# Key parts stored sooner, one bias waited for later, another loaded a stage earlier

## The chip, the cores and the metric

One core of one Trainium2 chip runs the whole program in one launch. The metric is the device time of that launch in microseconds (us); the time given for a kernel is the median over its runs.

## What is computed

Four pairs of layers on x (4 x 512 tokens, width 256): a cross attention against a second sequence `ctx`, then a feed-forward part. Each layer adds to x. What matters here are these three:

```
# L1 ffn: expert choice, 32 experts, each takes its top 8 of the rows of a (4, 32, 512) gating table
h = gelu(selected @ w1[e] + w1_last_row[e])        # 256 -> 1024
o = h @ w2[e] + w2_last_row[e]                     # 1024 -> 256, scattered back onto x
# keys of the L2 and L3 attentions depend on ctx alone
kL2 = rope(ctx @ WkL2.T);   kL3 = ctx @ WkL3.T + bk
# L3 attention: 16 heads of 16, values
v = ctx @ WvL3.T + bv
scores = scores * clip(exp(sqrt((tot - cumsum(softmax)) * |i-j|) * gamma * diff))
out = softmax(scores) @ v
```

## The kernel before

The program is written engine by engine with hand-set semaphores; each stage is a block that ends in a barrier of all engines. The order of the work on each engine is the order in which it is written. The stages stand in this order: attention L0x, experts L0f, attention L1x, experts L1f (`expert_choice`), attention L2x, experts L2f (`top2_experts`), distance attention L3x (`distance_layer`), feed-forward L3f.

**Stage L1f, the loop over experts.** 32 experts are taken in 8 groups g of 4. Each expert has two weights of 1024 KB, `w1s` in a ring of 8 buffers and `w2s` in a ring of 4. For each group PE computes `up(g)` (L2255), turns h (`turn`, L2268), and computes `down(g)` (L2281); ACT copies the left half of h (L2316) and applies Gelu (L2327); DVE copies the right half (L2347), adds the first bias (L2354) and, after `down(g)`, adds the second bias `b2` into `stage` (L2363). SP issues the loads: the `w2s` of group g once `down(g-1)` is done, then the `w1s` of group g+1 (L2100, L2096). The `w1s` of groups 0 and 1 and the `w2s` of group 0 were asked for in the stage's opening. `b2` (8 groups x 256 values for every partition, 1024 KB) is asked for when the loop begins, and DVE waits for it at the very beginning.

**Keys made beside it.** The class `LaterKeys` uses PE's free time for 16 jobs, the keys of L2x (jobs 0 to 7, rotated by angle) and of L3x (jobs 8 to 15). `project(j)` on PE; `take(j)` on ACT; `split(j)` on DVE writes two of three bf16 parts; `last_part(j)` on POOL writes the third (L2073) and signals `lo_done`; `store(j)` on ACT waits for `lo_done` and issues a DMA of 384 KB (L1998). The parts lie in a ring of 4, so `take(j)` (L2032) waits until the store of job j-4 has landed. Each group has at most three jobs:

```
between, first, second = ([None] * 5 + [9, 12, 15], [None, 1, 3, 5, 7, 10, 13, None],
                          [0, 2, 4, 6, 8, 11, 14, None])
```

`between[g]` is projected between `up(g)` and `turn(g)`, `first[g]` before `down(g)`, `second[g]` after it. Before the change ACT stores, in group g right after the copy of h, the jobs second[g-2], between[g-1] and first[g-1].

**The distance layer.** `norm_and_project` opens it: SP issues the load of the value bias `bv` and then of `wk` and `bk`; PE waits for `bv` before the first value product (L320), and ACT waits for `bv`, `wk` and `bk` before it issues four loads of 1024 KB into `apart` (L2862), whose sigmoids (L2872) it computes between copies. `distance_attention` then runs a software pipeline over 64 heads of 4 tiles each. Its small tiles (`nm1`, `rl`, `mx2`, `nm2`, `gate`, `v_sum_pair`, `pick`, `rdm`) each have memory of their own; each holds between 4 and 68 values a partition.

Of the kernel before, what the change touches and what calls it, by code (L numbers as in the profile page):

```python
# [2076 lines left out]
def expert_choice(c, ks2, ks3, wv2):  # L2077
# [6 lines left out]
    with ExitStack() as ctx:  # L2084
# [105 lines left out]
        with ExitStack() as ectx:  # L2190
# [20 lines left out]
            with nc.Block() as block:  # L2211
# [98 lines left out]
                def _(act):  # L2310
                    act.wait_ge(hT_cleared, 1)
                    for g in range(G):
# [4 lines left out]
                        if g:  # L2317
                            for j in (second[g - 2] if g > 1 else None, between[g - 1], first[g - 1]):
                                if j is not None:
                                    later.store(act, j)  # L2320
                            later.leading(act, second[g - 1])
# [3 lines left out]
                        if g >= 1:  # L2325
                            act.wait_ge(o_done, g)
                        nc.scalar.activation(hT[:, :, :, 0:B], hb[:], ACT.Gelu  # L2327
                                             ).then_inc(g_done, 1)
                        if first[g] is not None:
                            later.take(act, first[g])  # L2330
                            later.leading(act, first[g])
                        if second[g] is not None:
                            later.take(act, second[g])
                    later.store(act, second[G - 2])
                    later.store(act, between[G - 1])
# [4 lines left out]
                def _(dve):  # L2340
                    dve.wait_ge(b1_loaded, 16)
                    dve.wait_ge(b2_loaded, 16)
                    for g in range(G):
# [16 lines left out]
                        if between[g] is not None:  # L2360
                            later.split(dve, between[g])
                        dve.wait_ge(o_done, g + 1)
# [141 lines left out]
def top2_experts(c, wv3):  # L2504
# [14 lines left out]
    with ExitStack() as ctx:  # L2519
# [187 lines left out]
        with ExitStack() as gctx:  # L2707
# [8 lines left out]
            with nc.Block() as block:  # L2716
# [11 lines left out]
                def _(pe):  # L2728
# [3 lines left out]
                    pe.wait_ge(wv3_loaded, 16)  # L2732
# [182 lines left out]
def distance_attention(c, tag, stacks, vaug, o_dram, mask, apart, gamma, room_v, ahead):  # L2915
# [17 lines left out]
    with ExitStack() as ctx:  # L2933
        nm1 = c.sb(ctx, tag + "nm1", [P, F], F32)
        rl, mx2, nm2 = (c.sb(ctx, tag + n, [P, F], F32) for n in ("rl", "mx2", "nm2"))
# [38 lines left out]
        with nc.Block() as block:  # L2974
# [24 lines left out]
            def _(pe):  # L2999
# [43 lines left out]
                def turn_back(g, q):  # L3043

                    pe.wait_ge(oT_copied, g + 1)
                    for t in range(TB):
                        to = op[:, t * 2 * VW:(t + 1) * 2 * VW]
                        nc.tensor.matmul(to, oT[:, t * P:(t + 1) * P], pick[:].rearrange("p h d -> p (h d)"),
# [146 lines left out]
            def _(dve):  # L3195
# [50 lines left out]
                def invert(g):  # L3246

                    dve.wait_ge(o_done, g + 1)
                    nc.vector.reciprocal(rdm[:], o4[:, :, :, dk]).then_inc(rd_done, 1)

                def outputs(g):
# [6 lines left out]
                                                  rdm[:].unsqueeze(3).to_broadcast([P, TB, 2, dk]), ALU.mult)  # L3258
# [26 lines left out]
def distance_layer(c, ks, wv):  # L3285
# [6 lines left out]
    with ExitStack() as ctx:  # L3292
# [8 lines left out]
        with ExitStack() as wctx:  # L3301
# [3 lines left out]
            bv = c.sb(wctx, tag + "bv", [P, HD], F32)  # L3305
# [8 lines left out]
            def other_loads(sp):  # L3314
                sp.dma_start(bv[:], dram["L3_bv"].partition_broadcast(P)).then_inc(v_loaded, 16)
# [11 lines left out]
            def mask_terms(dve, made):  # L3327
# [4 lines left out]
                             (v_loaded, 16), None, (wk, wk, wv), (bks, bk, bv), 0.25, (qs, ks), vaug, dk + 1,  # L3332
# [3 lines left out]
        distance_attention(c, tag, stacks, vaug, o_dram, (mq, am, vsum), apart, gamma, wv, ahead)  # L3336
# [14 lines left out]
def build(nc, dram, out, layers):  # L3351
    with ExitStack() as ctx:
# [20 lines left out]
        if "L3x" in layers:  # L3373
            with ExitStack() as w_ctx:
                wv3 = c.sb(w_ctx, "L3x_wv", [P, KD, D], F32)
                top2_experts(c, wv3)
                c.end_layer()
                distance_layer(c, ks3, wv3)
# [101 lines left out]
```

## Time and profile before

| | us |
|---|---|
| median of 3 runs | 3150.31 |
| lowest and highest run | 3141.8, 3152.29 |
| the profiled execution | 3181.4 |
| its span, first to last instruction | 3179.6 |
| stage L1f within the span | 1288.4 to 1511.5 |
| opening of L3x within the span | 2307.2 to 2369.7 |

PE was busy 2735.3 us of the span (86%), DVE 1879.2 (59%), ACT 1720.9 (54%), POOL 851.0 (27%). Times in the rows are microseconds from the start of the span unless marked ns. PE is the matrix engine, PEld its weight loads, DVE the vector engine, ACT the scalar engine, POOL the general one; SPq and ACTq are the queues in which SP and ACT issue DMAs. L2281 is line 2281 of the kernel. "[3.67 <-PE ...]" at a row's end is the engine's idle time before it and what ended that.

### The profile page before, as it was taken

The numbers are of one execution on the slowest core, as the hardware profiler recorded it, in microseconds if no ns is written. First come the engines' busy times: TensorE is split into PE (matmuls) and PEld (weight loads), VectorE is DVE, ScalarE is ACT, GpSimd is POOL, SyncE is SP. The second block draws the span as 40 slices with busy tenths as digits, with TensorE's granted clock in tenths as the row PEclk, the third lists the DMA queues.
The fourth block names the chain that finished last, engine by engine and source line by source line (L and its number), as shares of the span: only waits on it lengthen the run. The fifth ranks groups of instructions, "written<-read, shape, count | busy, mean of one in ns | idle before, by whom it ended". The sixth has DMA issues, their size and how long they took to land. (4 is left out here: it accounts for less than half of the span.)

```text
span 3179.6 us, 43427 instructions
## 1 busy us (share of the span) xinstructions
PE 2735.3 (86%) x14726; PEld 1530.7 (48%) x14820; DVE 1879.2 (59%) x4756; ACT 1720.9 (54%) x2876; POOL 851.0 (27%) x957
## 2 busy tenths in 40 slices
PE   7899869869999999576699878999867888888887
PEld 3333349834444454232323246999633454444453
DVE  6777641165555655323688640111469999999953
ACT  3566421146555555111277631333149999999963
POOL 4010020020000000011300030000348888888840
PEclk9899989979999999787799999999978999999988
DMA  5111156510000000696212162999350000000001
GB/s 173 48 57 48 56 196 224 178 53 1 1 1 1 1 1 1 275 422 263 77 51 72 56 241 84 343 347 345 93 154 11 21 27 21 22 17 21 24 24 49
DMA packets 161834, 325.85 MB, mean 102 GB/s; under 512 B 29392, under 2 KB 128464, under 8 KB 138448
## 3 DMA queue, kind: packets, MB, share of 16 engines
q1 hardware_dynamic: 146384, 297.90, 27.2%
q0 software_dynamic: 4608, 12.59, 1.2%
q10 hardware_dynamic: 10624, 12.58, 1.1%
q8 instruction: 121, 1.98, 0.3%
q14 instruction: 97, 0.79, 0.1%
HBM read 273.71 MB, written 49.15 MB: 102 GB/s over the span
## 5 line engine op out<-in xcount | busy, mean ns | idle before, releaser
L3218 DVE TENSOR_TENSOR_SCAN L3x_behind<-L3x_first_exp,L3x_beside_scan 128x513 f32<-128x513 f32 x256 | 309.4, 1209 | 0.0
L3098 POOL TENSOR_TENSOR L3x_fade<-L3x_behind,L3x_apart 128x1024 f32<-128x1024 f32 x128 | 280.5, 2191 | 70.4 <-DVE L3x_behind L3218 47.5
L1369 ACT ACTIVATE L1x_probs<-L1x_scores,L1x_neg_max 128x512 f32<-128x512 f32 x256 | 173.7, 684 | 218.7 <-DVE L1x_neg_max L1421 218.7
L1421 DVE TENSOR_REDUCE L1x_neg_max<-L1x_scores 128x2 f32<-128x1024 f32 x128 | 156.6, 1224 | 143.8 <-PE L1x_scores L1269 143.8
L3136 ACT ACTIVATE L3x_first_exp<-L3x_scores,L3x_nm 128x512 f32<-128x512 f32 x256 | 229.3, 896 | 9.8 <-DVE L3x_nm L3210 9.7
L3164 ACT ACTIVATE L3x_probs_T<-L3x_probs_tp 128x512 f32<-128x512 f32 x256 | 204.7, 800 | 12.8 <-PE L3x_probs_tp L3026 12.3
L1696 ACT ACTIVATE L2f_hiddenT<-L2f_hidden_ps,L2f_b1s 128x128 f32<-128x128 f32 x312 | 97.6, 364 | 198.5 <-PE L2f_hidden_ps L1631 198.5
L814 DVE CUSTOM_DVE_ANT_0 L0x_masked_scores<-L0x_s,L0x_mask_q 128x512 f32<-128x512 f32 x256 | 167.0, 685 | 60.8 <-issue 54.3
L3144 ACT ACTIVATE L3x_fade<-L3x_fade,L3x_rl 128x512 f32<-128x512 f32 x256 | 199.2, 945 | 0.0
L809 DVE TENSOR_REDUCE L2x_neg_max<-L2x_s 128x1 f32<-128x512 f32 x256 | 164.7, 686 | 43.0 <-PE L2x_s L705 42.8
L3210 DVE TENSOR_REDUCE L3x_nm<-L3x_scores 128x1 f32<-128x512 f32 x256 | 172.8, 675 | 18.8 <-remote 17.4
L891 ACT ACTIVATE L0x_probs_T<-L0x_s 128x1024 f32<-128x1024 f32 x128 | 131.0, 1024 | 94.0 <-PE L0x_s L730 85.0
L3089 POOL TENSOR_SCALAR L3x_fade<-L3x_fade 128x1024 f32<-128x1024 f32 x64 | 178.1, 2783 | 5.5 <-ACT L3x_fade L3156 0.2
L3236 DVE CUSTOM_DVE_ANT_0 L3x_fade<-L3x_fade,L3x_scores_again 128x512 f32<-128x512 f32 x256 | 173.7, 679 | 5.7 <-issue 5.7
L3002 PE MATMUL L3x_scores<-L3x_k_stack,L3x_q_stack 96*128 96x512 bf16 x256 | 104.5, 408 | 80.9 <-ACT L3x_first_exp L3136 77.4
L2136 POOL MEMSET L1f_expert_tokens<- 128x2048 f32 x1 | 1.8, 1806 | 625.4 <-POOLq L141 625.4
L3023 PE MATMUL L3x_probs_tp<-identity,L3x_fade 128*128 128x128 f32 x1024 | 159.3, 279 | 10.8 <-POOL L3x_neg_max_parts L3107 8.3
L3023 PEld LDWEIGHTS L3x_probs_tp<-identity,L3x_fade 128*128 128x128 f32 x1024 | 128.3, 143 | 72.3 <-POOL L3x_neg_max_parts L3107 26.1
L1279 PEld LDWEIGHTS L1x_probs_tp<-identity,L1x_probs 128*128 128x128 f32 x1024 | 118.4, 142 | 83.7 <-issue 82.5
L3026 PE MATMUL L3x_probs_tp<-identity_bf,L3x_neg_max_parts 128*128 128x512 bf16 x512 | 156.5, 388 | 0.0
L891 ACT ACTIVATE L2x_probs_T<-L2x_s 128x1024 f32<-128x1024 f32 x128 | 130.9, 1024 | 46.7 <-PE L2x_s L727 45.2
L1380 ACT COPY L1x_probs_T<-L1x_probs_tp 128x512 f32<-128x512 f32 x256 | 137.6, 596 | 25.8 <-PE L1x_probs_tp L1279 24.2
(548 smaller groups left out, 6207.6 us busy)
## 6 DMA issues: line engine op xcount, KB each, us to landing
L2f_w1s<-in_L_w SPq DMA_DIRECT2D x39, 1024.0 KB
L2f_w2s<-in_L_w SPq DMA_DIRECT2D x39, 1024.0 KB
L1f_w1s<-in_L_w SPq DMA_DIRECT2D x32, 1024.0 KB, 18.3
L1f_w2s<-in_L_w SPq DMA_DIRECT2D x32, 1024.0 KB, 12.1
L0f_w1s<-in_L_w SPq DMA_DIRECT2D x16, 1024.0 KB, 6.2
L0f_w2s<-in_L_w SPq DMA_DIRECT2D x16, 1024.0 KB, 5.4
L0x_q_stack<-L0x_q_parts SPq DMA_DIRECT2D x96, 64.0 KB, 2.6
L0x_k_stack<-L0x_k_parts SPq DMA_DIRECT2D x96, 64.0 KB, 2.7
```

Of the source, the lines that this page charges most:

```text
L814: nc.vector.tensor_tensor_reduce(masked[:, t % 2, :], s1[:, t % 2, :], mq[:, t, :], 1.0, -3e38, ALU.add, ALU.max, smax[:, i % 2, t:t + 1]) ...
L891: nc.scalar.activation(pT[:, i, 2 * j:2 * j + 2, :], s2[:, j, :, :], ACT.Exp).then_inc(p_done, 1)
L1369: nc.scalar.activation(p[:, n % 3, h, :], s[:, n % 2, h, :], ACT.Exp, bias=nmax[:, n % 4, h:h + 1], accum_out=den[:, n % 4, h:h + 1]).then ...
L3023: nc.tensor.matmul(tp[:, t % 2, kt, :], fz[:, f, kt * P:(kt + 1) * P], c.ident[:], start=(kt == 0), stop=False, is_transpose=True)
L3089: nc.gpsimd.tensor_scalar(fz[:, f:f + 2, 0:S], fz[:, f:f + 2, 0:S], 1e-5, None, ALU.max).then_inc(clip2_done, 1)
L3098: nc.gpsimd.tensor_tensor(fz[:, f:f + 2, :], bs[:, fb:fb + 2, 0:S], w, ALU.mult).then_inc(y_done, 1)
L3136: nc.scalar.activation(ex[:, t, 1:S + 1], sA[:, t % 2, :], ACT.Exp, bias=nm1[:, f:f + 1]).then_inc(e_done, 1)
L3144: nc.scalar.activation(fz[:, f, 0:S], fz[:, f, 0:S], ACT.Ln, scale=rl[:, f:f + 1]).then_inc(ln_done, 1)
L3164: nc.scalar.activation(pT[:, i % 4, :, t * P:(t + 1) * P], tp[:, t % 2, :, :], ACT.Exp).then_inc(p_done, 1)
L3210: nc.vector.tensor_reduce(nm1[:, f:f + 1], sA[:, t % 2, :], AX.X, ALU.max, negate=True).then_inc(m_done, 1)
L3218: nc.vector.tensor_tensor_scan(bs[:, f, :], ex[:, t, :], beside[:, 0:1].to_broadcast([P, S + 1]), 0.0, ALU.add, ALU.bypass).then_inc(f_don ...
L3236: nc.vector.tensor_tensor_reduce(fz[:, f, 0:S], fz[:, f, 0:S], sB[:, t % 2, :], 1.0, -3e38, ALU.mult, ALU.max, mx2[:, f:f + 1]).then_inc(s ...
```

## The change

1. ACT in L1f: `store` of second[g-1] now follows the Gelu of group g, and the stores of between[g] and first[g] end group g. The same 16 stores are made, in other places.
2. DVE in L1f: the wait for `b2` moves from the loop's beginning to just before the first use of `b2` in group 0.
3. `bv` of L3x is loaded at the end of the loads of stage L2f into memory that lives on into L3x; the wait is at L2f's end. L3x's opening no longer loads it or waits for it.
4. Once the values are made, that memory (1 KB a partition) holds the eight small tiles of `distance_attention`.

```diff
                         if g:
-                            for j in (second[g - 2] if g > 1 else None, between[g - 1], first[g - 1]):
-                                if j is not None:
-                                    later.store(act, j)
                             later.leading(act, second[g - 1])
...
                         nc.scalar.activation(hT[:, :, :, 0:B], hb[:], ACT.Gelu
                                              ).then_inc(g_done, 1)
+                        if g:
+                            later.store(act, second[g - 1])
                         if first[g] is not None:
                             later.take(act, first[g])
                             later.leading(act, first[g])
                         if second[g] is not None:
                             later.take(act, second[g])
-                    later.store(act, second[G - 2])
-                    later.store(act, between[G - 1])
+                        for j in (between[g], first[g]):
+                            if j is not None:
+                                later.store(act, j)
...
                     dve.wait_ge(b1_loaded, 16)
-                    dve.wait_ge(b2_loaded, 16)
...
+                        if g == 0:
+                            dve.wait_ge(b2_loaded, 16)
                         dve.wait_ge(o_done, g + 1)
...
             sp.dma_start(wv3[:], dram["L3_wvT"].rearrange("(k p) n -> p k n", p=P)).then_inc(wv3_loaded, 16)
+            sp.dma_start(bv3[:], dram["L3_bv"].partition_broadcast(P)).then_inc(wv3_loaded, 16)
...
-                    pe.wait_ge(wv3_loaded, 16)
+                    pe.wait_ge(wv3_loaded, 32)
...
-        nm1 = c.sb(ctx, tag + "nm1", [P, F], F32)
-        rl, mx2, nm2 = (c.sb(ctx, tag + n, [P, F], F32) for n in ("rl", "mx2", "nm2"))
+        nm1, rl, mx2, nm2 = (room_b[:, n * F:(n + 1) * F] for n in range(4))
...
-        gate = c.sb(ctx, tag + "gate", [P, TB], F32)
+        gate = room_b[:, 13 * F:13 * F + TB]
...
-        vsu = c.sb(ctx, tag + "v_sum_pair", [P, 2, 2, VW], F32)
-        pick = c.sb(ctx, tag + "pick", [P, 2, VW], F32)
+        vsu = room_b[:, 4 * F:4 * F + 4 * VW].rearrange("p (q h d) -> p q h d", q=2, h=2)
+        pick = room_b[:, 9 * F:9 * F + 2 * VW].rearrange("p (h d) -> p h d", h=2)
...
-        rdm = c.sb(ctx, tag + "rdm", [P, TB, 2], F32)
+        rdm = room_b[:, 12 * F:12 * F + 2 * TB].rearrange("p (t h) -> p t h", h=2)
...
-                sp.dma_start(bv[:], dram["L3_bv"].partition_broadcast(P)).then_inc(v_loaded, 16)
+                pass
...
-                             (v_loaded, 16), None, (wk, wk, wv), (bks, bk, bv), 0.25, (qs, ks), vaug, dk + 1,
+                             (v_loaded, 0), None, (wk, wk, wv), (bks, bk, bv), 0.25, (qs, ks), vaug, dk + 1,
...
-                wv3 = c.sb(w_ctx, "L3x_wv", [P, KD, D], F32)
-                top2_experts(c, wv3)
+                wv3, bv3 = c.sb(w_ctx, "L3x_wv", [P, KD, D], F32), c.sb(w_ctx, "L3x_bv", [P, D], F32)
+                top2_experts(c, wv3, bv3)
```

On ACT, groups 6 and 7 of L1f (L2316 is the copy that begins a group, L2029 and L2032 are `take`, L2327 the Gelu, L1998 a store), before:

```order
L2316 COPY L1f_h<-L1f_hps 128x512
L1998 DMA L3x_k_parts<-L1f_later_parts 128x3x512 x3
L2029 ACTIVATE L1f_later_full<-L1f_later_acc,L1f_later_bk 128x512
L2032 ACTIVATE L1f_later_parts<-L1f_later_acc,L1f_later_bk 128x512
L2327 ACTIVATE L1f_hT<-L1f_hT_biased 128x32x4
L2029 ACTIVATE L1f_later_full<-L1f_later_acc,L1f_later_bk 128x512
L2032 ACTIVATE L1f_later_parts<-L1f_later_acc,L1f_later_bk 128x512
L2029 ACTIVATE L1f_later_full<-L1f_later_acc,L1f_later_bk 128x512
L2032 ACTIVATE L1f_later_parts<-L1f_later_acc,L1f_later_bk 128x512
L2316 COPY L1f_h<-L1f_hps 128x512
L1998 DMA L3x_k_parts<-L1f_later_parts 128x3x512 x3
```

and now:

```order
L2316 COPY L1f_h<-L1f_hps 128x512
L2029 ACTIVATE L1f_later_full<-L1f_later_acc,L1f_later_bk 128x512
L2032 ACTIVATE L1f_later_parts<-L1f_later_acc,L1f_later_bk 128x512
L2324 ACTIVATE L1f_hT<-L1f_hT_biased 128x32x4
L1998 DMA L3x_k_parts<-L1f_later_parts 128x3x512
L2029 ACTIVATE L1f_later_full<-L1f_later_acc,L1f_later_bk 128x512
L2032 ACTIVATE L1f_later_parts<-L1f_later_acc,L1f_later_bk 128x512
L2029 ACTIVATE L1f_later_full<-L1f_later_acc,L1f_later_bk 128x512
L2032 ACTIVATE L1f_later_parts<-L1f_later_acc,L1f_later_bk 128x512
L1998 DMA L3x_k_parts<-L1f_later_parts 128x3x512 x2
L2316 COPY L1f_h<-L1f_hps 128x512
```

The three stores of jobs 11, 12 and 13 (in group 6 before: of jobs 8, 9 and 10) no longer stand behind the next group's copy of h: 11 stands right behind the Gelu of group 6, 12 and 13 ahead of the copy of group 7.

On SP, the end of the loads of stage L2f, now (the row of L2542 is new; before, the same load stood first among SP's issues in L3x):

```order
L2804 DMA L2f_sb<-in_L_sb 128x256
L2541 DMA L3x_wv<-in_L_wvT 128x2x256
L2542 DMA L3x_bv<-in_L_bv 128x256
L141 UNCONDITIONAL_BRANCH
L2571 UNCONDITIONAL_BRANCH
L2575 DMA L2f_disp<-L2f_zero 128x2560 x4
```

One DMA issue moved from the opening of L3x to the opening of L2f.

## Rows read from the trace of the kernel before

**Rows 1.** The page, part 2, speed of the DMA engines in 40 slices of 79.5 us

```profile
GB/s 173 48 57 48 56 196 224 178 53 1 1 1 1 1 1 1 275 422 263 77 51 72 56 241 84 343 347 345 93 154 11 21 27 21 22 17 21 24 24 49
```

**Rows 2.** Waits, 1290 to 1500: waiter <- releaser: us, times, longest

```profile
ACT L1f_later_parts L2032 <- DMA L3x_k_parts<-L1f_later_parts: 15.0, 2, 7.6
...
DVE L1f_h L2347 <- DMA L1f_b<-in_L_w_last: 12.6, 1, 12.6
...
ACT L1f_later_parts L2032 <- DMA L2x_k_parts<-L1f_later_parts: 10.4, 3, 6.0
```

**Rows 3.** Timeline, start of the expert loop: start, duration, engine, line [idle before <-releaser]

```profile
1317.67 0.59 ACT L2316 COPY L1f_h<-L1f_hps 128x512 f32<-128x512 f32 x1 [14.08 <-PE L1f_hps L2255]
...
1318.21 4.84 SPq L2222 DMA_DIRECT2D L2x_wv<-in_L_wvT  x1
...
1325.93 0.69 DVE L2347 COPY L1f_h<-L1f_hps 128x512 f32<-128x512 f32 x1 [12.61 <-DMA L1f_b<-in_L_w_last]
...
1328.81 5.11 PE L2281 MATMUL L1f_ops<-L1f_w2s,L1f_hT 128*32 128x256 f32 x64 [1.01 <-ACT L1f_hT L2327]
...
1334.03 2.18 SPq L2100 DMA_DIRECT2D L1f_w2s<-in_L_w  x4
```

**Rows 4.** Windows: stretch, length, busy PE, PEld, DVE, ACT, POOL, PEclk, DMA share, GB/s

```profile
1326.00:1336.00 10.00, 8.31 (x76) 4.24 (x80) 1.53 (x6) 0.44 (x2) 0.00 (x0) 0.71 0.25 71
1336.00:1464.00 128.00, 89.82 (x626) 38.41 (x619) 34.30 (x77) 20.63 (x38) 24.07 (x21) 0.84 1.02 422
1465.00:1472.00 7.00, 7.00 (x69) 2.91 (x68) 1.04 (x3) 1.27 (x2) 0.00 (x0) 0.76 0.23 59
1473.00:1486.00 13.00, 6.12 (x44) 2.39 (x36) 2.20 (x7) 2.34 (x4) 1.81 (x2) 0.85 0.99 376
```

**Rows 5.** Timeline, last two groups of experts

```profile
1461.67 0.69 ACT L2032 ACTIVATE L1f_later_parts<-L1f_later_acc,L1f_later_bk 128x512 bf16<-128x512 f32 x1 [7.57 <-DMA L3x_k_parts<-L1f_later_parts]
...
1466.12 4.72 PE L2281 MATMUL L1f_ops<-L1f_w2s,L1f_hT 128*32 128x256 f32 x64
...
1470.92 3.05 SPq L2100 DMA_DIRECT2D L1f_w2s<-in_L_w  x4
...
1476.40 1.64 ACTq L1998 DMA_DIRECT2D L3x_k_parts<-L1f_later_parts  x3
...
1486.41 0.69 ACT L2032 ACTIVATE L1f_later_parts<-L1f_later_acc,L1f_later_bk 128x512 bf16<-128x512 f32 x1 [7.44 <-DMA L3x_k_parts<-L1f_later_parts]
...
1487.54 5.94 PE L2281 MATMUL L1f_ops<-L1f_w2s,L1f_hT 128*32 128x256 f32 x64 [8.43 <-ACT L1f_hT L2327]
```

**Rows 6.** DMA issues, 1250 to 1500: count, size, median us to landing

```profile
L1f_w2s<-in_L_w SPq DMA_DIRECT2D x32, 1024.0 KB, 12.1
...
L3x_k_parts<-L1f_later_parts ACTq DMA_DIRECT2D x8, 384.0 KB, 10.8
```

**Rows 7.** Timeline, third group of experts

```profile
1366.42 0.30 ACT L2327 ACTIVATE L1f_hT<-L1f_hT_biased 128x128 f32<-128x128 f32 x1
...
1367.71 3.66 PE L2281 MATMUL L1f_ops<-L1f_w2s,L1f_hT 128*32 128x256 f32 x64 [0.78 <-DMA L1f_w2s<-in_L_w]
1367.83 1.16 POOL L2073 TENSOR_TENSOR L1f_later_parts<-L1f_later_rest,L1f_later_parts 128x512 bf16<-128x512 f32 x1 [7.80 <-DVE L1f_later_parts L2063]
```

**Rows 8.** Timeline, opening of the distance layer

```profile
2307.20 0.34 SPq L3315 DMA_DIRECT2D L3x_bv<-in_L_bv  x1
...
2310.62 5.78 PE L320 MATMUL L3x_v_acc<-L3x_wv,context_T 128*128 128x256 f32 x16 [9.70 <-DMA L3x_bv<-in_L_bv]
...
2311.52 4.38 ACTq L2862 DMA_DIRECT2D L3x_apart<-in_pdiff  x4
...
2332.83 1.91 ACT L2872 ACTIVATE L3x_apart<-L3x_apart 128x2048 f32<-128x2048 f32 x1 [0.27 <-DMA L3x_apart<-in_pdiff]
```

**Rows 9.** Windows, steady part of the distance attention

```profile
2400.00:3040.00 640.00, 559.24 (x3244) 305.65 (x3302) 622.41 (x1438) 637.44 (x866) 547.38 (x656) 0.97 0.08 20
```

**Rows 10.** The page, part 5: count | busy, mean ns of one | idle before

```profile
L3136 ACT ACTIVATE L3x_first_exp<-L3x_scores,L3x_nm 128x512 f32<-128x512 f32 x256 | 229.3, 896 | 9.8 <-DVE L3x_nm L3210 9.7
```

More of the change, by code:

```diff
@@ L2501, in _, with top2_experts @@
                                                     ).then_inc(added, 1)
-def top2_experts(c, wv3):
+def top2_experts(c, wv3, bv3):
     nc, dram = c.nc, c.dram
@@ L2912, in tile_at, with distance_attention @@
     return (k + d if isinstance(k, int) else k + d if d else k), (i + d) % 8, tt
-def distance_attention(c, tag, stacks, vaug, o_dram, mask, apart, gamma, room_v, ahead):
+def distance_attention(c, tag, stacks, vaug, o_dram, mask, apart, gamma, room_v, room_b, ahead):
     nc = c.nc
@@ L3047, in turn_back @@
                         to = op[:, t * 2 * VW:(t + 1) * 2 * VW]
-                        nc.tensor.matmul(to, oT[:, t * P:(t + 1) * P], pick[:].rearrange("p h d -> p (h d)"),
+                        nc.tensor.matmul(to, oT[:, t * P:(t + 1) * P], pick.rearrange("p h d -> p (h d)"),
                                          start=True, stop=False)
@@ L3248, in invert @@
                     dve.wait_ge(o_done, g + 1)
-                    nc.vector.reciprocal(rdm[:], o4[:, :, :, dk]).then_inc(rd_done, 1)
+                    nc.vector.reciprocal(rdm, o4[:, :, :, dk]).then_inc(rd_done, 1)
                 def outputs(g):
@@ L3257, in outputs @@
                     one = nc.vector.tensor_tensor(to, o4[:, :, :, 0:dk],
-                                                  rdm[:].unsqueeze(3).to_broadcast([P, TB, 2, dk]), ALU.mult)
+                                                  rdm.unsqueeze(3).to_broadcast([P, TB, 2, dk]), ALU.mult)
                     one.then_inc(o_read, 1)
@@ L3282, in _, with distance_layer @@
                 run(dve, body)
-def distance_layer(c, ks, wv):
+def distance_layer(c, ks, wv, bv):
     nc, dram = c.nc, c.dram
@@ L3304, in distance_layer @@
             bks = c.sb(wctx, tag + "bks", [P, MT], F32)
-            bv = c.sb(wctx, tag + "bv", [P, HD], F32)
             mload = c.sem(tag + "mask_loaded")
@@ L3335, in distance_layer @@
                                 c.ctxT[:, 1, 2 * S:4 * S].rearrange("p (t d) -> p t d", d=HD))
-        distance_attention(c, tag, stacks, vaug, o_dram, (mq, am, vsum), apart, gamma, wv, ahead)
+        distance_attention(c, tag, stacks, vaug, o_dram, (mq, am, vsum), apart, gamma, wv, bv, ahead)
     ahead.run()
@@ L3374, in build @@
             with ExitStack() as w_ctx:
-                wv3 = c.sb(w_ctx, "L3x_wv", [P, KD, D], F32)
-                top2_experts(c, wv3)
+                wv3, bv3 = c.sb(w_ctx, "L3x_wv", [P, KD, D], F32), c.sb(w_ctx, "L3x_bv", [P, D], F32)
+                top2_experts(c, wv3, bv3)
                 c.end_layer()
-                distance_layer(c, ks3, wv3)
+                distance_layer(c, ks3, wv3, bv3)
                 c.end_layer()
```

## The prediction

> **What bounds the kernel now.** I read the page's speed of the DMA engines first [rows 1]. The only slices at 422 GB/s or near lie in stage L1f, where 32 experts' weights of 2 MB each are fetched: slices 17 to 19 (275, 422, 263). The reader should see that in this stage the program runs as fast as the DMA queue delivers. The windows say how steadily [rows 4]: from 1336 to 1464 the engines move 422 GB/s at a share of 1.02, while PE has work for 90 of 128 us. So an engine's wait inside that stretch is worth nothing by itself. What is worth something is time in which the queue is empty. There are two such holes: 1326 to 1336 (71 GB/s) and 1465 to 1472 (59 GB/s) [rows 4].
>
> The waits name their causes [rows 2]. The first hole: DVE sits 12.6 us until `b2` lands, before it copies the right half of h, though it needs `b2` only after `down(0)`. ACT had copied its half at 1317.67, DVE follows at 1325.93 [rows 3]. So `down(0)` starts at 1328.81, and the `w2s` of group 1, which wait for it, are asked for at 1334.03 [rows 3]; the queue has run dry meanwhile. The second hole: ACT waits 7.57 us (until 1461.67) for a store of keys to land before `take(12)`, which stands ahead of the Gelu of group 6. So `down(6)` starts at 1466.12, and the last `w2s` are asked for at 1470.92 [rows 5]. In group 7 it happens again: ACT waits 7.44 us for the store of job 11, issued at 1476.40, and `down(7)` starts at 1487.54 after an idle PE of 8.43 us, its wait named as the Gelu and not as weights [rows 5].
>
> **The change, part by part.**
>
> *The wait for b2.* DVE's copy can follow `up(0)` as ACT's did: at 1317.7 in place of 1325.93, 8.2 us sooner. `down(0)` moves from 1328.81 to about 1320.6, and with its 5.11 us ends near 1325.7 [rows 3]; that is about when `b2` lands, so DVE's addition of it, now behind the wait, is hardly held. SP is free from 1323.05 (1318.21 + 4.84) [rows 3] and asks for the `w2s` of group 1 near 1325.8. The queue's emptiness in the first hole is 10 x (1 - 71/422) = 8.3 us [rows 4], so what was asked for before lasts until 1336 - 8.3 = 1327.7. The new request is about 2 us ahead of that, which is about what lay between request (1334.03) and full flow (1336). So the stream of weights starts 8.3 us sooner. Bounds: 8.3 if the request is in time, 6 if `down(0)` runs wholly at 1.2 GHz like the 5.94 us of `down(7)` [rows 5] and the request then takes longer to bring bytes.
>
> *The stores of keys.* The same 16 stores, same 16 issues, on ACT. Each is asked for half a group to a group sooner. Job 11's stands right behind the Gelu of group 6, ahead of `down(6)` (1466.12), where it was issued at 1476.40 [rows 5]: more than 10 us sooner. Stores take 10.8 us in the median to land [rows 6], so it is there when ACT reaches `take(15)`, at 1486.41 - 7.44 = 1479.0. Job 8's store, which `take(12)` needs, moves ahead likewise. Both waits should go, and with them the second hole and the idle before `down(7)`. Late next are the weights themselves.
>
> What this costs: ACT now waits for POOL's last part at two places. Behind the Gelu of group 2 (1366.72) POOL is done at 1368.99 [rows 7]: 2.3 us in which `take(first)` is held. PE does not miss it, as it computes `down` from 1367.71 to 1371.37 [rows 7]. At a group's end POOL is done before PE has gone through the next `up(g)`, which waits for weights. I cost both at nothing; if the weights ever came early this cover would go, but then the stage would already be shorter.
>
> *The sum for the stage*, by volume. From its start the stream carries the `w2s` of groups 1 to 7 and the `w1s` of groups 2 to 7: 52 loads of 1024 KB = 54.5 MB. With them go the stores asked for ahead of the last load, 0.393 MB each: 11 before, now 11 to 15, I take 13 = 5.1 MB. 59.6 MB at 422 GB/s [rows 4] are 141.2 us; from 1327.7 on this gives 1468.9, and with 0.8 us from the last byte to the first product 1469.7. `down(7)` starts at 1487.54 now [rows 5]: **17.8 us gained**. Bounds: 11 stores 19.7, 15 stores 15.9; less 2.3 if the first term is at its low end; 2 more if `down(7)`, after a shorter idle time, runs at 2.4 GHz like the 3.66 us of [rows 7] and not in 5.94. The tail behind it, rows of `o` summed onto x, is unchanged, and the last stores land under it.
>
> A rule speaks against this sum. The Trainium skill, "DMA: Bandwidth & Descriptors", section Specifications, gives a limit of about 358 GB/s of HBM for one core; by it the 59.6 MB would take an estimated 166 us and `down(7)` would start at 1494, no sooner than now. The trace does not agree: it has 422 GB/s over 128 us of nothing but such transfers [rows 4], so I sum by the row and give that outcome no chance of its own. The trace shows 10.8 us in the median, so stores mostly land behind the weights they meet.
>
> *bv loaded in L2f.* There it is one more SP issue, 0.34 us [rows 8], at the end of a list of loads after which SP has to wait for others anyway: nothing. In L3x, PE now waits until 2310.62 for it and could begin at 2307.2, 3.4 us sooner [rows 8]. But ACT sets this stage's end: it waits for the four loads into `apart`, the last still ending a wait at 2332.83 [rows 8], and these are asked for once `wk` and `bk` land. Only SP's one issue less, 0.4 us, moves that. Bounds 0 and 3.4; I take **0.4**, as ACT's last wait is the nearer row.
>
> *Small tiles in one place.* No instruction is added or lost in `distance_attention`. ACT is busy 637.4 of 640 us there [rows 9], so it is the bound, and reads a column of such a tile with each exponential, 896 ns in the mean [rows 10]. No row shows a cost of where a tile lies. I take 0; the bound on both sides is in the third rival.
>
> Sum: 17.8 + 0.4 = 18.2 us. Against the profiled execution's own 3181.4 that is 3163.2. It is 31.1 above the median of the runs, and I take the same 18.2 off the median: 3150.3 - 18.2 = **3132.1 us**.
>
> **The rivals.** What a measurement of this kernel can tell from no change is about 0.3%, 9.5 us.
>
> First, *only the first hole closes*. A store lands behind whatever weights are in flight, 10.8 us [rows 6]; with the queue full to the end, it may land so late that ACT waits for it again and `down(6)` is held as now. For it: every wait for a store in [rows 2] arose with the queue full. Against: the stores are asked for 10 us and more ahead. It gives 8.3 + 0.4 = 8.7, 3141.6 us. A half of it (one of the two late waits stays, some 4 us of the tail's 9.5) gives 13, 3137 us.
>
> Second, *nothing is gained*: the first hole does not close because something else asked for behind `b2` holds group 0, and the tail is held by a wait that is now hidden. Against: PE's product in the hole waits only for `b1`, h and weights long there. About 3150 us.
>
> Third, *slower*. ACT is the bound of 640 us [rows 9], and eight small tiles that three engines write and read now share 1 KB. If ACT's reads of columns there collided with the others' writes, each of its 512 exponentials of a tile would be longer. From 18.2/512 = 36 ns on, the gain is eaten; from 54 ns on it is slower by over 0.3%. At 60 ns: 31 us lost, 3163 us. For it: this instruction is the stage's bound. Against: four of these tiles (`nm1`, `rl`, `mx2`, `nm2`) were allocated one after the other before too.
>
> **How the numbers follow.** The forecast, a gain of 14 to 24 us, gets 0.62; the half 0.14; the first hole alone 0.14; nothing 0.05; slower 0.05. Faster by over 0.3%: the first two and a third of the third, 0.81; within: 0.14; slower 0.05. The forecast's own range is 3126 to 3136. The range down to 3123 takes in the faster PE and a median that sits as the lowest run did (3141.8, 8 below the median); up to 3143 it takes in the half and the first hole alone. Left out are nothing, slower, and a margin of measurement.
>
> **What would show it.** In the profile of the changed kernel: DVE's first copy of h with ACT's, 8 us ahead of the first `down`'s old place; no stretch like that of 71 GB/s behind it; no wait of ACT's `take` for a store of over 1 us in the last two groups; `down(7)` waiting for weights, about 18 us sooner; in L3x, PE's first value product at the stage's beginning and the fourth sigmoid only 0.4 us nearer to it; the exponential still 896 ns. A hole of DMA ahead of the last `w2s` would prove the tail's step wrong; an exponential of over 930 ns the last one.

## The result and the profile after

| | before | changed |
|---|---|---|
| median, us | 3151.3 (4 runs) | 3131.69 (4 runs) |
| lowest and highest | 3141.8, 3154.42 | 3129.3, 3133.23 |
| ratio, 95% interval | | 0.9942, 0.9919 to 0.9965 |
| the profiled execution, its span | 3181.4, 3179.6 | 3129.3, 3127.4 |

The time falls by 19.6 us; the forecast was 3132.1. The interval in us is a gain of 11 to 26.

The two profiled executions differ by 52 us, and most of that is not the change. The stage lengths show what is, each from the first row of a stage to the first of the next (the first row of L3x before is the load of `bv` at 2307.20 [rows 8]):

| stretch | before | changed |
|---|---|---|
| L0x, L0f, L1x and opening of L1f, together | 1313.6 | 1314.3 |
| L1f, from the load of `b2` to the start of L2x | 198.8 | 181.7 |
| L2x | 335.4 | 335.5 |
| L2f to SP's first load of scattered rows | 108.4 | 85.4 |
| L2f, the rest | 351.0 | 342.2 |
| L3x to its first scan | 69.5 | 67.1 |
| the scan loop of L3x, first scan to last | 670.2 | 668.7 |

L1f gives 17.1 us and L3x's opening 2.4. The 23.0 and 8.8 us in L2f belong to the execution: profiles without the change have the short stage too, and profiles with it the long one, as the experiments show.

**The first hole.** The timeline of the changed kernel at the start of the expert loop (columns as in [rows 3]):

```profile
1318.36 0.58 ACT L2316 COPY L1f_h<-L1f_hps 128x512 f32<-128x512 f32 x1 [14.10 <-PE L1f_hps L2255]
1318.37 0.69 DVE L2346 COPY L1f_h<-L1f_hps 128x512 f32<-128x512 f32 x1 [4.36 <-PE L1f_hps L2255]
...
1321.10 3.66 PE L2281 MATMUL L1f_ops<-L1f_w2s,L1f_hT 128*32 128x256 f32 x64 [1.01 <-ACT L1f_hT L2324]
1324.87 2.17 SPq L2100 DMA_DIRECT2D L1f_w2s<-in_L_w  x4
1326.41 0.42 DVE L2364 TENSOR_TENSOR L1f_stage<-L1f_ops,L1f_b 128x256 f32<-128x256 f32 x1 [5.79 <-DMA L1f_b<-in_L_w_last]
...
1329.44 3.48 PE L2010 MATMUL L1f_later_acc<-context_T,L1f_later_wk 128*128 128x512 f32 x4 [4.68 <-DMA L1f_later_bk<-in_L_bk]
```

DVE now copies with ACT, and the `w2s` are asked for 9.2 us sooner than in [rows 3]. The wait for `b2` has moved to the addition, where it is 5.79 us and holds nothing but `stage`. A new wait of 4.68 us has appeared on PE, for the small loads asked for behind `b2`. It comes after `down(0)`, so the request is already out.

**The second hole.** The windows of the changed kernel (columns as in [rows 4]), with that of the last `w2s` at the end:

```profile
1316.00:1326.00 10.00, 7.00 (x96) 3.76 (x87) 1.18 (x5) 2.18 (x3) 0.11 (x1) 1.00 1.01 413
1326.00:1336.00 10.00, 6.56 (x36) 2.12 (x36) 0.42 (x1) 0.58 (x1) 1.28 (x1) 0.83 1.03 420
1336.00:1448.00 112.00, 83.24 (x604) 36.04 (x596) 33.09 (x75) 19.93 (x37) 21.70 (x19) 0.89 1.02 422
1448.00:1460.00 12.00, 6.15 (x70) 3.06 (x68) 2.57 (x5) 2.64 (x4) 3.24 (x3) 0.95 1.02 422
1460.00:1468.00 8.00, 7.52 (x36) 2.21 (x37) 0.69 (x1) 0.58 (x1) 0.00 (x0) 0.65 1.02 420
1468.00:1472.00 4.00, 1.61 (x14) 1.09 (x16) 1.51 (x6) 1.57 (x3) 0.90 (x1) 1.00 0.77 299
```

There is no window like the 71 and 59 GB/s of [rows 4]; the queue runs full from 1316 to the last weights. The timeline of the last two groups (compare [rows 5]):

```profile
1448.95 0.37 ACTq L1998 DMA_DIRECT2D L3x_k_parts<-L1f_later_parts  x1
1449.18 3.66 PE L2281 MATMUL L1f_ops<-L1f_w2s,L1f_hT 128*32 128x256 f32 x64 [0.61 <-DMA L1f_w2s<-in_L_w]
...
1452.89 1.75 SPq L2100 DMA_DIRECT2D L1f_w2s<-in_L_w  x4
...
1460.48 6.17 PE L2255 MATMUL L1f_hps<-L1f_w1s,L1f_expert_tokens 128*32 128x512 f32 x32 [5.72 <-DMA L1f_w1s<-in_L_w]
...
1469.18 0.68 ACT L2032 ACTIVATE L1f_later_parts<-L1f_later_acc,L1f_later_bk 128x512 bf16<-128x512 f32 x1
...
1471.82 5.35 PE L2281 MATMUL L1f_ops<-L1f_w2s,L1f_hT 128*32 128x256 f32 x64 [2.39 <-DMA L1f_w2s<-in_L_w]
```

The store of job 11 goes out at 1448.95, 20.2 us before `take(15)` at 1469.18, which has no wait at its row's end where [rows 5] have 7.44 us. `down(7)` now waits for weights and starts at 1471.82. The waits of the changed kernel, 1290 to 1500, say the same (waiter <- releaser: us, times, longest). No wait of ACT for a store is left, and PE's waits for weights have taken its place.

```profile
PE L1f_hps L2255 <- DMA L1f_w1s<-in_L_w: 26.9, 6, 5.7
...
ACT L1f_later_plain L2026 <- POOL L1f_later_parts L2073: 11.1, 4, 2.8
PE L1f_ops L2281 <- DMA L1f_w2s<-in_L_w: 9.6, 6, 2.6
...
ACT L1f_later_full L2029 <- POOL L1f_later_parts L2073: 4.9, 2, 2.5
```

**L3x.** The timeline of its opening in the changed kernel (compare [rows 8]):

```profile
2259.13 6.26 PE L320 MATMUL L3x_v_acc<-L3x_wv,context_T 128*128 128x256 f32 x16 [5.64 <-PEq L70]
...
2262.04 4.81 ACTq L2864 DMA_DIRECT2D L3x_apart<-in_pdiff  x4
...
2282.51 1.91 ACT L2874 ACTIVATE L3x_apart<-L3x_apart 128x2048 f32<-128x2048 f32 x1 [0.28 <-DMA L3x_apart<-in_pdiff]
```

The stage starts at 2259.1. PE begins at once; ACT asks for `apart` 3.0 us after the start, where it was 4.3 (2311.52 - 2307.20), and the fourth sigmoid comes 23.4 us after the start, where it was 25.6. Part 5 of the page has the exponential:

```profile
L3137 ACT ACTIVATE L3x_first_exp<-L3x_scores,L3x_bv 128x512 f32<-128x512 f32 x256 | 235.1, 918 | 9.9 <-DVE L3x_bv L3211 9.7
```

The exponential takes 918 ns against the 896 of [rows 10], yet the scan loop took 1.5 us less. The experiments look into that.

### The profile page after: what moved, and what is told of

It is laid out like the page before. It is cut to its first block and busy times, and to the rows that moved or that the text cites. A ratio compares the mean times of both kernels' runs of the same rounds, so it can differ in the third digit from the quotient of the medians.

```text
span 3127.4 us, 43426 instructions
## 1 busy us (share of the span) xinstructions
PE 2723.5 (87%) x14726; PEld 1526.8 (49%) x14820; DVE 1880.2 (60%) x4756; ACT 1718.7 (55%) x2876; POOL 850.6 (27%) x957
## 5 line engine op out<-in xcount | busy, mean ns | idle before, releaser
L3099 POOL TENSOR_TENSOR L3x_fade<-L3x_behind,L3x_apart 128x1024 f32<-128x1024 f32 x128 | 280.9, 2194 | 68.5 <-DVE L3x_behind L3219 44.9
L3137 ACT ACTIVATE L3x_first_exp<-L3x_scores,L3x_bv 128x512 f32<-128x512 f32 x256 | 235.1, 918 | 9.9 <-DVE L3x_bv L3211 9.7
L3165 ACT ACTIVATE L3x_probs_T<-L3x_probs_tp 128x512 f32<-128x512 f32 x256 | 212.5, 831 | 11.3 <-PE L3x_probs_tp L3027 11.2
L3145 ACT ACTIVATE L3x_fade<-L3x_fade,L3x_bv 128x512 f32<-128x512 f32 x256 | 203.0, 975 | 0.0
L3211 DVE TENSOR_REDUCE L3x_bv<-L3x_scores 128x1 f32<-128x512 f32 x256 | 172.8, 675 | 17.5 <-remote 15.8
```

The source lines that it names most:

```text
L3099: nc.gpsimd.tensor_tensor(fz[:, f:f + 2, :], bs[:, fb:fb + 2, 0:S], w, ALU.mult).then_inc(y_done, 1)
L3137: nc.scalar.activation(ex[:, t, 1:S + 1], sA[:, t % 2, :], ACT.Exp, bias=nm1[:, f:f + 1]).then_inc(e_done, 1)
L3145: nc.scalar.activation(fz[:, f, 0:S], fz[:, f, 0:S], ACT.Ln, scale=rl[:, f:f + 1]).then_inc(ln_done, 1)
L3165: nc.scalar.activation(pT[:, i % 4, :, t * P:(t + 1) * P], tp[:, t % 2, :, :], ACT.Exp).then_inc(p_done, 1)
L3211: nc.vector.tensor_reduce(nm1[:, f:f + 1], sA[:, t % 2, :], AX.X, ALU.max, negate=True).then_inc(m_done, 1)
```

## The experiments

They ran in three sets, each kernel beside the kernel before on the same chip. In the second set that chip took 3184.23 us for the kernel before, so only ratios and differences within one set count.

| run | what it is | median, us | before beside it | ratio, 95% interval |
|---|---|---|---|---|
| e1_stores | before, stores moved | 3142.32 | 3150.32 | 0.9976, 0.9965 to 0.9986 |
| e2_b2_wait | before, wait for `b2` moved | 3141.31 | 3150.32 | 0.9973, 0.9964 to 0.9982 |
| e3_bv_tiles | changed, both edits of L1f undone | 3147.88 | 3150.32 | 0.9995, 0.9986 to 1.0004 |
| e4_tiles_only | before, small tiles together | 3147.66 | 3150.32 | 0.9992, 0.9983 to 1.0001 |
| e5_b2_twice | changed, 1 MB more to load | 3168.11 | 3184.23 | 0.9959, 0.9945 to 0.9972 |
| e6_apart_sooner | changed, `apart` asked for first | 3165.12 | 3184.23 | 0.9947, 0.9933 to 0.9960 |
| e7_b2_rows | changed, 0.9 MB less to load | 3168.49 | 3184.23 | 0.9954, 0.9940 to 0.9967 |
| e8_after | the changed kernel | 3129.56 | 3150.06 | 0.9938, 0.9924 to 0.9952 |
| e9_apart_again | as e6 | 3130.97 | 3150.06 | 0.9936, 0.9923 to 0.9950 |

e0_before, the kernel before, was run once for its profile, 3178.36 us.

**The edits of L1f, each alone.** e1 is the kernel before with this edit:

```diff
-                            for j in (second[g - 2] if g > 1 else None, between[g - 1], first[g - 1]):
-                                if j is not None:
-                                    later.store(act, j)
...
+                        if g:
+                            later.store(act, second[g - 1])
...
+                        for j in (between[g], first[g]):
+                            if j is not None:
+                                later.store(act, j)
```

> The kernel before with the moved stores alone. My theory: the stage of the 32 experts is a stream of weights at 422 GB/s with two holes, and this closes the second alone. The first hole stays as wide as it was (DVE's first copy of h behind the wait for b2), no take waits for a store of over 1 us in the last two groups, the last down starts some 9 to 10 us sooner in the profile, and the median falls by 9 to 10 us. Rival: the stores still land too late with a full queue, or the second hole was only there because the first had put the groups late: then less than 3 us.

e2 is the kernel before with this one:

```diff
-                    dve.wait_ge(b2_loaded, 16)
...
+                        if g == 0:
+                            dve.wait_ge(b2_loaded, 16)
```

> The kernel before with DVE's wait for b2 moved alone. My theory: the first hole closes, 8 us, and the rest of the stage moves as a whole: takes still wait 6 to 8 us for stores in the last groups and the queue still runs dry ahead of the last loads. The median falls by 7 to 9 us. Rival: the tail has its own clock, so that an earlier stream only makes the waits in the tail longer: then under 4 us, and the two edits are worth more together than one by one.

e1 gained 8.0 us where 9 to 10 were expected, e2 9.0 where 7 to 9 were. From the load of `b2` to L2x the stage took 190.7 us in e1 and 188.9 in e2, against 198.8 and 195.5 in the two profiles of before and 181.7 with both. Two more profiles with L1f as before, e3 and e4, have 196.1 and 199.0, so the four without either edit average 197.4, and the 17.1 us of the first pair lie at the upper end. Against that mean e1 gained 6.7, e2 8.5 and both together 15.7. Each closes its own hole and leaves the other. The windows of e1, the first hole and the stretch where the second was:

```profile
1326.00:1336.00 10.00, 7.10 (x64) 3.91 (x68) 1.17 (x5) 0.31 (x1) 0.00 (x0) 0.51 0.32 112
...
1464.00:1470.00 6.00, 0.98 (x3) 0.15 (x1) 0.57 (x2) 1.37 (x2) 1.15 (x1) 0.92 1.03 424
```

and the timeline of e2's last two groups:

```profile
1442.15 1.45 ACTq L1998 DMA_DIRECT2D L3x_k_parts<-L1f_later_parts  x3
1455.29 0.69 ACT L2032 ACTIVATE L1f_later_parts<-L1f_later_acc,L1f_later_bk 128x512 bf16<-128x512 f32 x1 [10.58 <-DMA L3x_k_parts<-L1f_later_parts]
...
1459.74 3.72 PE L2281 MATMUL L1f_ops<-L1f_w2s,L1f_hT 128*32 128x256 f32 x64
...
1478.06 0.69 ACT L2032 ACTIVATE L1f_later_parts<-L1f_later_acc,L1f_later_bk 128x512 bf16<-128x512 f32 x1 [6.47 <-DMA L3x_k_parts<-L1f_later_parts]
...
1479.20 5.91 PE L2281 MATMUL L1f_ops<-L1f_w2s,L1f_hT 128*32 128x256 f32 x64 [7.46 <-ACT L1f_hT L2327]
```

With the first hole closed, ACT's wait before `take(12)` grew from 7.57 [rows 5] to 10.58 us, while that before `take(15)` fell from 7.44 to 6.47: weights come sooner, and the stores still go out late. So the rival "only the first hole closes" is just what e2 alone does, and it is the moved stores that keep it from being the whole result. The two add up (8.0 and 9.0 in the medians, 19.6 and 20.5 for all four edits) because both are empty time of one queue, at two places. e1 also shows how far the first term can move: there PE's `down(0)` took 6.54 us, at a granted clock of 0.51 in its window, in before 5.11; in every kernel with the wait for `b2` moved it took 3.66.

**The edits of L3x.** e3 is the changed kernel with L1f as before. e4 has only the small tiles together, in a tile of their own:

```diff
-        nm1 = c.sb(ctx, tag + "nm1", [P, F], F32)
-        rl, mx2, nm2 = (c.sb(ctx, tag + n, [P, F], F32) for n in ("rl", "mx2", "nm2"))
+        room_b = c.sb(ctx, tag + "room_b", [P, HD], F32)
+        nm1, rl, mx2, nm2 = (room_b[:, n * F:(n + 1) * F] for n in range(4))
...
+        gate = room_b[:, 13 * F:13 * F + TB]
```

> The changed kernel with both edits of the stage of 32 experts undone, so bv loaded a stage earlier and the small tiles in its memory. The profile of the changed kernel had the opening of the distance layer 2.4 us shorter, not 0.4. My theory: the load of bv held up wk and bk, behind which ACT's four large loads are asked for; the opening is 2 to 2.5 us shorter here too, the distance loop the same within 2 us, the median 2 to 4 us lower. Rival (the step as predicted): 0.4 us, and the rest of what the profile showed is the spread between two executions.

> The kernel before with nothing changed but that the eight small tiles of the distance attention lie in one tile of 1 KB. My theory: no difference in time (within 3 us), and ACT's exponential as in the kernel before, 896 ns in the mean within 1%; the 918 ns of the changed kernel's profile then come from the timing of the engines against each other. Rival: ACT's reads collide with writes nearby: its exponentials are longer by 20 ns or more each here too, and the loop of the distance attention is longer by up to 5 us.

Both medians are some 2.5 us below before's, and both intervals hold 1. So e3's median cannot be put down to `bv`: e4, without the early bias, is as far below. The profiles say more. In the five profiles of kernels that load `bv` in L3x (before, e0, e1, e2, e4) the stretch from the stage's start to the first scan takes 69.5, 68.2, 68.1, 68.1, 68.5 us, mean 68.5; in the five that load it early and are otherwise alike there (changed, e3, e5, e7, e8) 67.1, 66.4, 66.6, 68.3, 67.0, mean 67.1. So the early bias is worth about 1.4 us in the mean; the 68.3 of e7, within the other group, shows how far one profile can stray. ACT's request for `apart` goes out 4.0 to 4.3 us after the start in the first group and 2.9 to 3.1 in the second. The scan loop takes 669.4 us in e3 and 669.6 in e4, 670.1 to 670.4 in the four kernels with the tiles apart and 668.7 to 670.6 in all eight with them together: the tiles' place costs nothing. Part 5 of the pages of e2 and e4, tiles apart and tiles together:

```profile
L3137 ACT ACTIVATE L3x_first_exp<-L3x_scores,L3x_nm 128x512 f32<-128x512 f32 x256 | 225.4, 881 | 9.8 <-DVE L3x_nm L3211 9.7
```

```profile
L3136 ACT ACTIVATE L3x_first_exp<-L3x_scores,L3x_room_b 128x512 f32<-128x512 f32 x256 | 226.0, 883 | 9.9 <-DVE L3x_room_b L3210 9.7
```

The mean goes from 881 to 899 ns with the tiles apart and from 883 to 918 with them together, over twelve profiles, and the loop's length does not follow it. (e4 was expected within 1% of 896 and has 883.) Only one of the eight profiles with the tiles together is above 902; since e8, the same kernel, has 892, the 918 was the execution's.

**Volume.** Two kernels ask whether the stage is now a matter of bytes. e5 loads `b2`'s 1 MB a second time, e7 only those 16 of `b2`'s 128 partitions that hold values which are used, the rest cleared by POOL:

```diff
+                    sp.dma_start(stage[:], dram["L1_w2_last"]).then_inc(b2_loaded, 16)
```

```diff
-                    sp.dma_start(b2[:], dram["L1_w2_last"]).then_inc(b2_loaded, 16)
+                    sp.wait_ge(b2_cleared, 1)
+                    for q in range(4):
+                        sp.dma_start(b2[q * W:q * W + B, :, :], dram["L1_w2_last"][q * W:q * W + B]).then_inc(b2_loaded, 16)
...
+                    nc.gpsimd.memset(b2[:], 0.0).then_inc(b2_cleared, 1)
```

> The kernel before once more, for a second profile: in the first the stage of the top-2 experts (from its first load to the first load of the distance layer) was 460 us, in the profile of the changed kernel 428, with no edit there but one load. My theory: the 32 us are of that one execution, as its time lay 31 us above the median; here that stage takes 427 to 435 us. Rival: the change shortens it: 455 to 465.

> The changed kernel with 1 MB more brought by the same queue right behind b2 (b2's values a second time, into the memory of the staged results, before they are written). My theory: after the change the length of the expert stage is set by the bytes of its stream alone, so 1.05 MB at 422 GB/s cost 2.5 us. Rival: the stage is held by a chain of engines: under 1 us.

> The changed kernel with only the 16 partitions of b2 that are used brought (131 KB in four loads; the rest is cleared by POOL), 0.92 MB less in the stream. My theory (bytes set the stage): 2.2 us faster than the changed kernel. Rival: the four narrow loads, behind a wait for POOL, cost SP's queue more than they save.

The second profile of before did not do what was expected. L2f took 458.5 us in it, in the rival's range of 455 to 465, where the theory said 427 to 435: it was no matter of that one execution. The rival is wrong all the same: e1, e2 and e4, which leave L2f as before, have 427.6 to 430.1, and e5, e6 and e7, which load `bv` there, have 459.8 to 461.3. The long L2f goes with the chip or the occasion, not with the edit.

The edits of e5 and e7 leave L3x as in the changed kernel; that of e6 beside them (below) shortens it by some 1.5 us. e5 took 3.0 us more than e6, and 3.7 more from the load of `b2` to L2x (185.3 against 181.6). Of these 1.0 is a slower `down(7)` (6.34 us against 5.35). The start of `down(7)` is the cleaner measure: it came 182.7 us after the stage's start in the changed kernel, e6, e8 and e9 alike, and 185.5 in e5. That is 2.8 more, where 1 MB at 422 GB/s is 2.5, so the extra bytes cost about their volume. e7 gained nothing: 3.4 us above e6, and from the start of L1f to L2x 209.9 us, against 207.0 in e6 and 206.9 in the changed kernel. Of these 3.0 us, 1.1 are `down(7)`'s own length and 1.8 its start. (Its profiled execution took 3174.17, 5.7 above its median.) Its windows and rows of its timeline show why:

```profile
1326.00:1336.00 10.00, 7.20 (x88) 3.52 (x84) 0.42 (x1) 0.59 (x1) 1.02 (x1) 1.00 1.05 313
1336.00:1464.00 128.00, 91.44 (x684) 39.28 (x674) 35.65 (x80) 22.48 (x41) 25.24 (x22) 0.88 1.02 422
```

```profile
1325.76 3.66 PE L2285 MATMUL L1f_ops<-L1f_w2s,L1f_hT 128*32 128x256 f32 x64 [1.01 <-ACT L1f_hT L2328]
...
1329.53 2.59 SPq L2100 DMA_DIRECT2D L1f_w2s<-in_L_w  x4
```

The next `w2s` can be asked for only when `down(0)` is done. With less of `b2` in the queue it runs low before that (313 GB/s, and 363 from 1318 to 1326), so the bytes saved come back as emptiness. The stage's length then follows the request. From the request to `down(7)` e7 took 146.3 us, and the changed kernel, e6, e8 and e9 took 146.5 to 147.0, although e7 had 0.92 MB less to bring. The request went out 38.2 us after the stage's start (1291.3), in the changed kernel 35.8. That lateness is a matter of PE, which began `up(0)` 0.8 us later and took 5.29 us for it instead of 3.64, and no row ties that to the edit. The expectation's rival, the wait for POOL, is there too: SP asked for `b2` 28.8 us after the start instead of 25.2. It may have deepened the emptiness, but it did not delay the request, as SP was free at 1324.69. A run of e7 with PE in time might end level with the changed kernel. In the changed kernel the request (1324.87) comes just as the queue runs out: it moves 413 GB/s from 1316 to 1326 and 420 behind it. So `b2` is the cover of `down(0)`.

**One more step in L3x.** e6 asks for `apart` before ACT waits for `wk` and `bk`:

```diff
                     wait_pos(act, *v_loaded)
+                    loads[2](act)
                     act.wait_ge(*k_loaded)
-                    loads[2](act)
```

> The changed kernel with ACT's four large loads of the distance layer asked for before, not after, its wait for wk and bk. ACT can begin them 1.5 us after the stage's start instead of 2.95. My theory: the opening's end hangs on when the last of these lands, so the opening is shorter by 1 to 1.4 us. Rival: these loads now slow wk and the mask down and PE's projections take over: no gain.

The request went out 1.1 us after the stage's start and the opening took 65.6 us, 1.5 less than the mean of the five others with an early bias (0.8 to 2.7 less than each). That is about the theory's size. Its time could not be read without the changed kernel beside it, so both ran again:

> The changed kernel with the four apart loads asked for before ACT waits for wk and bk, the same kernel as e6_apart_sooner, now beside the changed kernel itself. In e6's profile the requests went out 1.1 us after the stage's beginning instead of 2.9 to 3.1, and the stretch to the first scan took 65.6 us where the others with an early bias had 66.4 to 67.1. The theory (the landing of the apart loads sets the end of the opening) expects 1.0 to 1.8 us less than e8_after. The rival, that something else (the keys' query projections) sets the end, expects the same time as e8_after within a few tenths.

> The changed kernel itself, beside the kernel before and beside the next one. The theory (the gain is the sum of the two closed holes and some 1 to 2.5 us of L3x, whatever the level at which a chip runs) expects a gain of 17 to 20 us here too: 0.994 of before, whether before shows some 3150 or some 3184. If the higher level of the second set of runs (3184) comes from 23 us of stillness in the routing part of L2f, as the profiles of that level show it (108.9 us from the start of L2f to its scatter, against 85.4), then this profile shows 85.4 when its time is near 3131 and 108.9 when it is near 3165. The rival is that the gain hangs on the level: then it would be some 20% smaller or larger at the higher one. The exponential of the distance attention is expected anywhere between 881 and 918 ns, as in the eight profiles so far, with no sign that it belongs to the tiles' place; the scan loop 668 to 671 us.

The opening was 65.0 us in e9 and 67.0 in e8, 2.0 less, and yet the medians are 3130.97 and 3129.56. The profile of e9 has 338.1 us in L2x where e8's has 335.2, a step between two levels that before's two profiles show as well (335.4 and 337.8), with the same code there. So the opening is shorter in both profiles of this kernel, and the gain is not seen in the time, where 1.0 to 1.8 us were expected; no kernel here beats the changed one.

e8 confirms the result: 20.5 us gained. On the chip of the higher level e6, the nearest to it there, gained 19.1: the gain does not hang on the level. The level itself sits in one place. From L2f's start to SP's first load of scattered rows (the expectation of e8 below says "to its scatter") the profiles of the second set's chip have 108.9 us (e0, e5, e6, e7) and before's first 108.4; those of the other two chips have 85.4 to 85.6 (e1 to e4, e8, e9), as has the changed kernel's. The waits in that stretch, of before and of e8:

```profile
ACT L2f_shT L2820 <- PE L2f_shps L2810: 55.5, 18, 37.9
...
DVE L2f_y L2840 <- issue: 29.1, 1, 29.1
DVE L2f_y L2840 <- remote: 14.3, 1, 14.3
...
PE L2f_sops L2829 <- issue: 10.0, 1, 10.0
```

```profile
DVE L2f_y L2842 <- PE L2f_sops L2831: 51.1, 8, 16.8
ACT L2f_shT L2822 <- PE L2f_shps L2812: 36.6, 22, 14.9
```

In before DVE stands 29.1 us at one instruction and 14.3 at another, and PE 10.0, and the trace names no engine and no DMA that ends these waits. Not all of the 29.1 is extra. In the changed kernel the same instruction waits 16.2 us for PE's product. It comes 46.9 us after the stage's start there and 59.8 in before, and the three like it behind it take another 10.1 us longer: together the 23.0 us. These waits lie within, or end just behind, the time in which POOL issues the 32 scatter DMAs (1876.9 to 1917.8 in before). The profiles of the lower level have the same 32 DMAs beside the same work, so that alone is no cause. With 5 to 10 us more in the rest of L2f, and in most profiles 2 to 3 in L2x, this makes up the 31 to 34 us between the levels. What holds them was not tried.

## Why the prediction was right, point by point

**The wait for b2.** The mechanism is as predicted. DVE's copy came at 1318.37 (1317.7 was said, the stage began 0.7 later), `down(0)` at 1321.10, the request at 1324.87 (1325.8), b2's addition at 1326.41. The size of `down(0)` was off: 5.11 us was taken, 3.66 came, because PE no longer idles 8 us before it and its granted clock is 1.00 in that window instead of 0.71: 2.4 GHz throughout instead of in part. The request was sooner for it and the stream was not, since the queue still held work. The bound of 6 us did not arise. Its reading was off as well: it took the 5.94 us of `down(7)` as wholly at 1.2 GHz, where the window 1487.6 to 1493.4 has a granted clock of 0.60, and e1's `down(0)` took 6.54 at 0.55.

**The stores.** Both waits and the second hole went, as said. e2 shows that without this edit the wait would have grown to 10.58 us; e1 that alone it is worth 8 us. The 10.8 us taken for a store's landing was too kind: it is the median over all of L3x's stores, and those issued from 1326 to 1472, beside full weights, took 16.1 in before and 15.2 in the changed kernel. The step held because job 11's store left 20.2 us ahead of `take(15)`.

**ACT's waits for POOL.** They came, 11.1 us in four and 4.9 in two, the longest 2.8, where 2.3 was read for one. PE waited 1.0 us in all for a `take`, where before it was 13.8; they cost nothing.

**The sum by volume.** It gave 1469.7 for `down(7)`; the row has 1471.82, of which 0.7 is the later start of the loop. The rest is within the bounds: 14 stores passed ahead of the end of the stream, not 13 (the DMA issues, 1326 to 1472, list eight of L2x's and six of L3x's), which is 0.9 us. Measured from the stage's start `down(7)` came 16.4 us sooner, where 17.8 was said. From the load of `b2` on, the stretch gained 17.1 us; 0.6 of that is `down(7)` itself, 5.35 us in place of 5.94. In e8 `down(7)` ran at 2.4 GHz, in 3.66 us, and the stretch took 179.1, which is the "2 more" of the bounds.

**The two rules.** The windows again have 420 to 422 GB/s, now over 142 us; the figure of 358 that the prediction took from the Trainium skill, "DMA: Bandwidth & Descriptors", section Specifications, does not hold here. The prediction should have read on: the Trainium skill's page "HBM Reference", section Specifications (TRN2), says that a core streaming alone measures about 425 GB/s and that the lower figure is the share when both cores of a domain stream. One core ran here, and the trace agrees with that sentence. The estimate of 4 us for a store's landing by turns of packets was far off. The DMA issues of the changed kernel, 1250 to 1500:

```profile
L2x_k_parts<-L1f_later_parts ACTq DMA_DIRECT2D x8, 384.0 KB, 12.4
L3x_k_parts<-L1f_later_parts ACTq DMA_DIRECT2D x8, 384.0 KB, 14.5
```

The estimate took equal bytes for each queue, as far as can be told: a store's 0.393 MB at half of 422 GB/s take 1.9 us, and the prediction does not say what the rest of its 4 is. The two queues' rows, 1326 to 1472 (packets, MB, share of 16 engines), show how unlike their packets are:

```profile
q1 hardware_dynamic: 8494, 55.45, 90.4%
q10 hardware_dynamic: 5600, 5.51, 10.7%
```

A packet of ACT's queue carries 1.0 KB (5.51 MB by 5600), one of SP's 6.5. Taking turns, if the profile's packets are those of the rule, ACT's queue would get 13% of 422 GB/s and a store an estimated 7 us: nearer, and still half of what is seen.

**bv.** The term was mis-sized: 0.4 us was taken, within bounds of 0 and 3.4; the profiles have about 1.4 in the mean and 2.4 in the first pair. The step that fell short was "Only SP's one issue less, 0.4 us, moves that". Without `bv` ahead of them `wk` and `bk` also land sooner, 2.5 to 2.8 us after their issue instead of 3.1 to 3.4, and ACT's request follows 1.4 us sooner in the first pair. The sign "the fourth sigmoid only 0.4 us nearer" failed with it: it came 2.2 us nearer. The choice of the path was right: e6 and e9 move the end by moving that same request.

**Small tiles.** Nothing, as said. But the sign given for it, an exponential of over 930 ns, was poor. The mean moves by 37 ns between executions without any effect on the loop. ACT is 638 of 640 us busy, and still a profile with a longer exponential has no longer loop. So "it is the bound" was not shown by the busy share, and the price of 18.2/512 put on the third rival rested on it.

**The sum and the level.** 18.2 us was taken off the median, although the profiled execution stood 31.1 above it. That was safe because the difference lay in L2f, outside both places of the change. The prediction did not look where it lay, and one profile of before could not have shown it; nor could e0, which has the same long stretch. It took a profile of a kernel like before at its median, such as e4's.

**The near hit.** 3132.1 was said and 3131.69 measured. The mechanism was right, but a distance of 0.4 us is luck: the interval of the gain is 11 to 26 us, the stage's term was 1.4 too large by the first pair, the term of `bv` about 1.0 too small, and the runs of one kernel spread over 4 to 13 us.

## What to carry to other kernels

Where a queue is the bound, list the stretches in which it is empty, find for each the instruction whose end permits the next request, and move only what delays that instruction; such gains add up, as 8.0 and 9.0 us did here. A wait for something not yet needed costs as if it were work when a request stands behind it. Saving bytes can be worth nothing where they cover the time until the next request, as in e7: check that before making a load smaller.

## What the hardware showed that was not expected

The level of the time depends on the chip or the occasion by 34 us (3150 against 3184 us for the same kernel), of which 23.5 us sit in one stretch of L2f, in waits of DVE (29.1 and 14.3 us in before) and PE (10.0) for which the trace names no engine and no DMA. One profile of a kernel can therefore be 1% from another's for a reason that has nothing to do with the edit; stage lengths tell it.

The same exponential took 881 to 918 ns in the mean, and the loop in which ACT has hardly a gap took 668.7 to 670.6 us, the shortest with the longest exponential. ACT's two other large groups of 512 columns vary with it, from 788 to 831 and from 932 to 975 ns. What the longer time of the instruction holds was not found out.
